# Cross-attention on one Trainium2 core: the products for the maxima made from three of six partial products, two heads in the two halves of TensorE's rows

## What is computed

```python
qh, kh, vh = split_heads(q @ wq.T + bq), split_heads(k @ wk.T + bk), split_heads(v @ wv.T + bv)   # 16 heads of 16
scores = einsum('bhqd,bhkd->bhqk', qh, kh) / sqrt(16)        # 512 queries, 1024 keys
attn = softmax(where(mask == 0, -1e9, scores))
out = einsum('bhqk,bhkd->bhqd', attn, vh) ... @ wo.T + bo
```

## Time and profile before

| | us |
|---|---|
| median of 3 runs | 1036.03 |
| lowest and highest | 1030.18, 1039.89 |
| the profiled execution | 1033.9 |
| its span, first to last instruction | 1032.1 |
| PE busy, all stages | 909.1 (88%) |
| DVE busy | 644.1 (62%) |
| ACT busy | 468.8 (45%) |
| POOL busy | 321.6 (31%) |
| c stage, from its first DMA issue (141.5) to the next stage's (400.8) | 259.3 |
| h stage, likewise (726.8 to 899.4) | 172.6 |

### The profile page before, as it was taken

How to read it: one execution, slowest core, us unless ns; L and a number is a source line. 1 busy time by engine, 2 the same in 40 slices (tenths; PEclk the granted TensorE clock), 3 DMA queues, 4 the chain that set the end, 5 groups by cost and what they waited for, 6 DMA issues and landing times. The chain is left out here.

```text
span 1032.1 us, 12736 instructions
## 1 busy us (share of the span) xinstructions
PE 909.1 (88%) x4040; PEld 460.9 (45%) x4044; DVE 644.1 (62%) x1329; ACT 468.8 (45%) x926; POOL 321.6 (31%) x328
## 2 busy tenths in 40 slices
PE   5879888999999986599799999999979998639986
PEld 2435553333333235366655555555422332434565
DVE  4855667888899824455145555654698996545464
ACT  3776444677777761022133333332207777133321
POOL 7325536300000000265235454553320000116633
PEclk9989998999999997699799999999988999859998
DMA  5040036033224704433590000000200000093100
GB/s 150 1 152 1 1 67 97 1 48 48 48 48 104 270 1 144 191 123 103 173 388 0 1 1 1 0 1 1 77 3 17 32 17 1 24 341 111 32 16 25
DMA packets 41654, 73.77 MB, mean 71 GB/s; under 512 B 8965, under 2 KB 27781, under 8 KB 40437
## 3 DMA queue, kind: packets, MB, share of 16 engines
q1 hardware_dynamic: 36372, 59.68, 19.4%
q0 software_dynamic: 4400, 13.11, 3.9%
q10 hardware_dynamic: 816, 0.17, 0.1%
HBM read 49.67 MB, written 10.49 MB: 58 GB/s over the span
## 5 line engine op out<-in xcount | busy, mean ns | idle before, releaser
L1066 DVE TENSOR_REDUCE c_amx<-PS 128x1 f32<-128x512 f32 x256 | 158.7, 682 | 29.9 <-PE PS L966 29.7
L1158 ACT ACTIVATE c_aE<-PS 128x512 f32<-128x512 f32 x256 | 132.5, 602 | 47.0 <-PE PS L978 46.9
L1782 POOL TENSOR_SCALAR s_Pn<-s_Pr,s_rs 128x512 f32<-128x512 f32 x64 | 100.1, 1567 | 107.4 <-DVE s_rs L1810 107.2
L68 POOL TENSOR_SCALAR rstd<-mv 128x4 f32<-128x4 f32 x8 | 1.9, 233 | 342.7 <-DVE mv L91 342.6
L966 PE MATMUL PS<-c_aKs,c_aQs 99*128 99x512 bf16 x256 | 95.8, 386 | 6.6 <-DMA c_aQs<-area 3.5
L978 PE MATMUL PS<-c_aQs,c_aKs 99*128 99x512 bf16 x256 | 94.5, 380 | 3.5 <-ACT c_aE L1158 2.3
L1869 ACT ACTIVATE s_Pr<-PS,s_nmx 128x512 f32<-128x512 f32 x64 | 44.0, 688 | 116.2 <-DVE s_nmx L1803 116.2
L1801 DVE TENSOR_REDUCE s_mx<-PS 128x1 f32<-128x512 f32 x64 | 44.2, 691 | 69.0 <-PE PS L1917 69.0
L1066 DVE TENSOR_REDUCE h_amx<-PS 128x1 f32<-128x512 f32 x128 | 79.7, 682 | 9.1 <-PE PS L966 8.8
L1158 ACT ACTIVATE h_aE<-PS 128x512 f32<-128x512 f32 x128 | 67.9, 600 | 23.6 <-PE PS L978 23.2
L989 PE MATMUL PS<-c_aE,c_VB 128*17 128x512 f32 x512 | 67.4, 598 | 0.1
(11 more groups left out here) (438 smaller groups left out, 1686.3 us busy)
## 6 DMA issues: line engine op xcount, KB each, us to landing
area<-in_e_w SPq DMA_DIRECT2D x16, 512.0 KB, 9.4
area<-in_g_w SPq DMA_DIRECT2D x8, 1024.0 KB, 16.4
c_aKs<-area SPq DMA_DIRECT2D x48, 128.0 KB
g_B<-in_g_b SPq DMA_DIRECT2D x1, 4096.0 KB, 16.2
c_aQs<-area SPq DMA_DIRECT2D x48, 64.0 KB
h_aQs<-h_QP SPq DMA_DIRECT2D x48, 64.0 KB
early<-in_ctxT SPq DMA_DIRECT2D x2, 1024.0 KB, 8.1
e_B<-in_e_b SPq DMA_DIRECT2D x1, 2048.0 KB, 11.3
```

The source lines that it names most:

```text
L1066: dve.tensor_reduce(self.mx[:, qt, j, half:half + 1], PS[:, n % MB, :], AX.X, ALU.max).then_inc(self.max_done, 1)
L1158: act.activation(self.E[kt % 2][:, j, :], PS[:, MB + x % XB, :], ACT.Exp, scale=0.25).then_inc(self.exp_done, 1)
L1782: pool.tensor_scalar(Pn[g % NPB][:, :], Pr[g % NPB][:, :], rs[:, g % NPB:g % NPB + 1], None, ALU.mult).then_inc(pn_ready, 1)
```

## The change

`Qs` and `Ks` become 115 rows high, and there are two layouts (`STACKS`). Heads 0 and 1 of a unit use the first, with the three partial products of slots 0, 3 and 4 and the tails in rows 0 to 50 and the rest up to row 98. Heads 2 and 3 use the second, with the same in rows 64 to 114, the others in rows 16 to 63 and zeros in rows 0 to 15. `scores` contracts only rows 0 to 50 or 64 to 114. It takes the heads in the order 0, 2, 1, 3 and issues them in pairs ahead of two `transposed_scores`, which contract 99 or 115 rows. Every DMA for the tails, keys and queries becomes two, one for each layout, with half of the partitions (32 instead of 64) and two heads. POOL sets the zero rows at the start of each stage. In the h stage the keys are laid out twice: DVE makes 9 copies instead of 2 after the splitting, PE 8 transposes instead of 4, ACT one copy of 1024 columns instead of 512. `MB` and `XB` are as before. What is left is the order of heads and dimensions in the weights (`dim_major`), which costs nothing on the chip.

```diff
+class Stack:
+    def __init__(self, slots, tail, main, rows):
+        self.slots, self.tail, self.main, self.rows = slots, tail, main, rows
+    def slot(self, n):
+        return slice(self.slots[n], self.slots[n] + HD)
+STACKS = (Stack((0, 35, 51, 16, 67, 83), slice(32, 35), slice(0, 51), slice(0, 99)),
+          Stack((64, 99, 16, 80, 32, 48), slice(96, 99), slice(64, 115), slice(0, 115)))
+PAIR = 2
+ROWS = 115
+HEAD_ORDER = (0, 2, 1, 3)
...
+def pair_rows(g, t):
+    first = g % 2 * 64 + t * 32
+    return slice(first, first + 32)
@@ Attention.tensor
-        def scores(u, c, j):
-            n = (u * C + c) * GH + j
+        def scores(u, c, i):
+            n = (u * C + c) * GH + i
+            j = HEAD_ORDER[i]
+            rows = stack_of(j).main
...
             if n >= MB:
                 pe.wait_ge(self.max_done, n - MB + 1)
-            pe.matmul(PS[:, n % MB, :], self.Qs[u % self.NQ][:, j, qt * P:(qt + 1) * P],
-                      self.Ks[self.key_buffer(u)][:, j % self.KH, half * BANK:(half + 1) * BANK],
+            pe.matmul(PS[:, n % MB, :], self.Qs[u % self.NQ][rows, j, qt * P:(qt + 1) * P],
+                      self.Ks[self.key_buffer(u)][rows, self.key_head(j), half * BANK:(half + 1) * BANK],
                       start=True, stop=True).then_inc(self.s_done, 1)
...
                 for j in range(GH):
-                    if v is not None:
-                        scores(v, c, j)
+                    if v is not None and j % PAIR == 0:
+                        for i in range(j, j + PAIR):
+                            scores(v, c, i)
                     transposed_scores(u, kt, j)
...
+    def set_zeros(self, pool, stacks, n):
+        for t in stacks:
+            pool.memset(t[0:HD, pair_heads(1), 0:n], 0.0).then_inc(self.zeros_set, 1)
@@ Attention.vector
-            for j in range(GH):
-                n = (u * C + c) * GH + j
+            for i, j in enumerate(HEAD_ORDER):
+                n = (u * C + c) * GH + i
@@ cross_stage, SP
             def key_part(u, p):
                 b, g = divmod(u, NG)
-                src = KP[p][g % 2 * 64:g % 2 * 64 + 64, b, g // 2, :]
                 for slot in KEY_SLOTS[p]:
-                    sp.dma_start(at.Ks[u % 3][slot * HD:(slot + 1) * HD, :, :], src).then_inc(at.loaded[u % 3], 16)
+                    for t, stack in enumerate(STACKS):
+                        sp.dma_start(at.Ks[u % 3][stack.slot(slot), pair_heads(t), :],
+                                     KP[p][pair_rows(g, t), b, g // 2, :]).then_inc(at.loaded[u % 3], 16)
@@ cross_stage, POOL
+            at.set_zeros(pool, at.Qs, S)
+            at.set_zeros(pool, at.Ks, NK)
@@ hard_cross_stage, POOL
-            pool.memset(KS[:, :, TAIL:TAIL + 2], 1.0).then_inc(ends_set, 1)
-            pool.memset(KS[:, :, TAIL + 2:ROWS + 1], 0.0).then_inc(ends_set, 1)
+            pool.memset(KS[:, :, :, :], 0.0).then_inc(ends_set, 1)
+            pool.wait_ge(ends_set, 2)
+            for t, stack in enumerate(STACKS):
+                first = stack.tail.start
+                pool.memset(KS[:, t, :, first:first + 2], 1.0).then_inc(ends_set, 1)
+            at.set_zeros(pool, at.Qs, S)
@@ hard_cross_stage, DVE, take_found
+                own.link(dve.tensor_tensor(third, KR[:, i, :], second, ALU.subtract))
+                for p, part in enumerate((first, second, third)):
+                    for t, stack in enumerate(STACKS):
+                        for slot in KEY_SLOTS[p]:
+                            if (t, slot) != (0, p):
+                                dve.tensor_copy(KS[:, t, i, stack.slot(slot)], part).then_inc(ks_ready, 1)
@@ hard_cross_stage, PE, found_keys
-                for i in range(TB):
-                    last = pe.transpose(key_bank(b)[:, i * P:(i + 1) * P], KS[:, b * TB + i, 0:ROWS], sh.identb[:, :])
+                for t in range(len(STACKS)):
+                    for i in range(TB):
+                        last = pe.transpose(key_bank(b)[:, t * S + i * P:t * S + (i + 1) * P], KS[:, t, b * TB + i, 0:ROWS],
+                                            sh.identb[:, :])
```

More of the change, by code:

```diff
@@ L972, in transposed_scores @@
             n = (u * KT + kt) * GH + j
+            rows = stack_of(j).rows
+            if u == 0 and kt == 0 and j == 0:
+                pe.wait_ge(self.zeros_set, self.zeros)
             if kt == 0:
@@ L977, in transposed_scores @@
                 pe.wait_ge(self.exp_done, n - XB + 1)
-            pe.matmul(PS[:, MB + n % XB, :], self.Ks[self.key_buffer(u)][:, j % self.KH, kt * P:(kt + 1) * P],
-                      self.Qs[u % self.NQ][:, j, :], start=True, stop=True).then_inc(self.st_done, 1)
+            pe.matmul(PS[:, MB + n % XB, :], self.Ks[self.key_buffer(u)][rows, self.key_head(j), kt * P:(kt + 1) * P],
+                      self.Qs[u % self.NQ][rows, j, :], start=True, stop=True).then_inc(self.st_done, 1)
         def values(u, kt):
@@ L3194, in layouts @@
     one = 0x3F80
[L3195 removed]
+    A["q_tail"] = np.repeat(np.array([[0], [0], [one]], np.uint16), PAIR * S, 1)
     A["ctxT"] = I["ctx_1024"].transpose(2, 0, 1).reshape(KD, P, -1).transpose(1, 0, 2)
```

75 lines of the change are left out of this document (41 added, 34 removed).

## The result

The changed kernel takes 1067.57 us (median of 4 runs, 1064.56 to 1068.48), the kernel before 1037.09 (4 runs): 1.030 times as long, 95% interval 1.024 to 1.035. The forecast was 1072, its own range 1062 to 1080. The profiled execution took 1068.48 us, its span is 1066.7, so 34.6 more than the span before.

The account below looks back on a forecast made before the run. PE sets the pace, with DVE 0.33 us a step to spare. Terms 13.9 + 1.7 + 9.5 + 8.6 + 2.3 = 36.0 on 1033.9 gave 1069.9, with 2.1 for the median 1072; own range 1062 to 1080, with rivals 1047 to 1084.

Parts of the forecast that it names:

- The chain of the three banks: Plain step: fourth product waits for the step's first maximum, starts at t + 1.17; step 3.00 us instead of 2.81.
- Overlap of the pairs, and a turn of 0.107: Products for the maxima: paired products run side by side; each switch between row layouts costs PE 0.107 us.
- Steps, 13.9: c and h steps: 50 on-time steps 9.0 us, 32 late ones 3.2, 16 new turns 1.7; 13.9 in all.
- Prologue of the c stage, 1.7: c prologue: same chain, two turns more for each of eight, 1.7 us.
- Start of the c stage, 9.5: c start: 24 issues at an unchanged 0.64 us each move the whole stage by 9.5 us.
- Waits for loads, 8.6: Later c units: loads take 20.8 us including 3.1 to land, exceeding their windows; PE waits 8.6 us.
- the forecast's sign of waits in units 1 to 5: c stage: DMA waits of 0.5 to 3 us expected ahead of the last steps of units 1 to 5.
- The h stage's one-offs, 2.3: h keys: seven more DVE copies and a link, four more transposes, ACT's longer copy; 2.3 us for two batches.
- halved issues: Rival, SP's DMAs: an issue with half the partitions costs half; 1056 us, chance 0.15.
- No overlap: Rival, products for the maxima: pairs do not run side by side, 7 us more; 1079 us, chance 0.08.
- DVE's pace: Rival, plain steps: fourth product not held, DVE sets the pace; 1024 us with halved issues, else 1040 or more; chance 0.06.
- Turns and issues both cheap: Rival, steps and DMAs: chain right, but layout turns and DMA issues cost little; 1045 us, chance 0.05.

Follow-up runs that it names:

- e5_half_max_after: Changed kernel with each maximum taken over 256 of the 512 columns of its product; 1050.26 us.
- e3_three: Changed kernel with the step order pair, three transposed products, pair, one transposed product, values; 1059.37 us.
- e6_half_max_before: Kernel before the change with each maximum taken over 256 of the 512 columns of its product; 1022.75 us.
- e1_full_rows: Changed kernel with the products for the maxima contracting all 99 or 115 rows, order in pairs kept; 1059.06 us.
- e4_late_zeros: Changed kernel with POOL's memsets moved behind the work DVE does at the start of a stage; 1061.93 us.
- e10_best: Changed kernel with the order of e3_three, the zeros of e4_late_zeros, and the second layout's loads of units 0 and 3 to 7 issued from POOL; 1056.06 us.
- e11_held: e10_best with the semaphores for POOL's DMAs taken ahead of all stages; 1057.17 us.
- e13_first_zeros: e11_held with full rows, maxima and transposed products by turns, and the first buffers' zeros set ahead; 1045.94 us.

## Why the prediction was right, step by step

- *The chain of the three banks* (fourth product at t + 1.17, plain step 3.00). Right: 1.17 and 3.01 in the profile; e5_half_max_after freed it by DVE alone (2.75), e3_three by the order alone (2.80), and e6_half_max_before showed that it didn't bind before.
- *Overlap of the pairs, and a turn of 0.107.* Right: two products in 0.39, and 0.32 from a pair to the transposed products in after, where e1_full_rows has 0.22 between the same matmuls. "TensorEngine Tiling (Array Packing)" of the Trainium skill, Key Properties, has a change of tiling mode drain the engine. The rows show 0.10 to 0.11 a turn, in the first stage and in the c stage, less than waiting for a matmul of 0.39 to end would cost; the measurement decides here.
- *Steps, 13.9.* Measured 13.1: 10.7 in the c steps less 1.3 of waits for loads, and 3.7 in the h steps (4.9 less 1.2 in the first, which belongs to the second batch's keys). Plain steps gave 0.20 instead of 0.18, but there are only 31 of 2.81 or 2.82 in the kernel before and not 50, so they gave 6.1 and not 9.0. The others gave 7.0 where 3.2 and 1.7 were forecast: the late steps, taken at 0.1 of 0 to 0.32, gave 0.01, 0.11, 0.12 and 0.30, and the four with late values 0.30 each. That the term came out is partly luck.
- *Prologue of the c stage, 1.7.* Measured 2.7. One round takes 3.41 instead of 3.12, 0.30 for two turns and what they push, where two turns at 0.107 were 0.21. The rest is at its ends.
- *Start of the c stage, 9.5.* Measured 9.1: an issue of 32 partitions takes 0.64 as one of 64 does. Within it two errors cancel, which is luck. The landing, from the end of SP's last issue to PE's load, was 1.46 instead of 3.1, and SP waited 1.2 for the first parts, since DVE was held back.
- *Waits for loads, 8.6.* The term that was mis-sized. Only the last steps of units 4 and 5 were longer than in the other units, by 0.8 and 0.5, so 1.3. The windows were right (20.45 for unit 3, forecast 20.35) and so was SP's time (18.55 with its slow issues, forecast 17.7). Wrong were the 3.1 to land, read off the start of the stage. The last step of unit 4, in after:

```profile
328.61 1.23 SPq L1478 DMA_DIRECT2D c_aQs<-area  x2
...
331.23 0.10 PEld L998 LDWEIGHTS PS<-c_aKs,c_aQs 51*128 51x128 bf16 x2 [1.70 <-DMA c_aQs<-area]
```

SP's last issue ended at 329.84, the load went 1.39 later. In the last steps of units 1 to 3 the loads still had 0.5 to 1.0 to spare, so the forecast's sign of waits in units 1 to 5 came for two of the five. A wait that the profile puts down to a DMA need not cost anything: of the 1.70 here 0.85 is there in every plain step.
- *The h stage's one-offs, 2.3.* Measured 6.3: 5.1 at the start and 1.2 in the first step. The doubled keys account for some 2 of it, as forecast; 4.1 are POOL's memsets against DVE, a term that had been given "0 to 2" and counted as 0. e4_late_zeros took 4.1 away. The h stage as a whole is 8.2 longer, where the sign said 6.
- The rest, +2.1, is scatter of untouched parts.

Sum of the measured terms: 13.1 + 2.7 + 9.1 + 1.3 + 6.3 = 32.5, forecast 36.0. So the chain, the overlap and the cost of an issue were right, and the total of 1067.6 stands as near to 1072 as it does by luck as well: two terms missed in opposite directions, 7.3 too much and 4.0 too little, and the untouched parts added 2.1. The rivals: halved issues (1056) fell with the row of six issues in 3.86. No overlap (1079) fell with the pair in 0.39. DVE's pace (1024 or 1040) fell with the fourth product at t + 1.17. "Turns and issues both cheap" (1045) fell with both.

## What to carry to other kernels

Before a matmul is made shorter, look for what the next one waits for: with three banks and a maximum of 0.62, the fourth product starts 1.17 after the first whatever PE saves, and all that is moved behind it goes onto the path. Changing the layout so that each DMA moves half as much doubles the queue's time, because an issue costs the same 0.64; and a queue with little room left turns what is won in the steps into waits (5.9 of 7.6 us in e3_three). A memset on an idle engine is free only if no neighbour shares its way to memory: look at what runs beside it, not only at what its own engine does next.

## What the hardware showed that I had not expected

**POOL's memsets and DVE.** All instructions of the normalising line, in after and before, and of POOL's zeros in after. Columns: durations min/median/max in ns, first and last start.

```profile
L1538 DVE TENSOR_SCALAR X<-X,mv,rstd x8: 396/1080/1966, 143.3 to 152.6; 128x256 f32<-128x256 f32 x8
```

```profile
L1491 DVE TENSOR_SCALAR X<-X,mv,rstd x8: 394/398/652, 141.5 to 145.3; 128x256 f32<-128x256 f32 x8
```

```profile
L1092 POOL MEMSET c_aQs<- x3: 941/1085/1088, 143.3 to 145.2; 16x1024 bf16 x3
L1092 POOL MEMSET c_aKs<- x3: 1934/1934/1936, 146.2 to 150.0; 16x2048 bf16 x3
```

DVE's instruction alone takes 398 ns. Beside the memsets its median is 1080 and its longest 1966. Five of the eight start 0.04 to 0.12 us after a memset has started and end some 0.15 after it ends, so each of these waits for a whole one (1085 and 1934). The memsets lose as well: three take 3.01 beside DVE and 2.72 alone (e4_late_zeros). DVE's instructions that read PSUM are not slowed: those behind the first normalising take 1.39 for two in e3_three, with a memset running, and 1.40 in e4_late_zeros without one. The page "SBUF — State Buffer" of the Trainium skill, section "SBUF: two separate sides", has DVE and GpSimd share a pair of ports under an exclusive lock, held for the whole instruction; of DVE's instructions with one SBUF input it says so for those in a 2-port mode. The rows agree with the lock; which mode these instructions were in, no row shows.

**Issues from POOL are cheaper than from SP, and a stage's end is dearer.** 0.50 against 0.64 us an issue for the same DMA, and 7 us at the end of the stage in the four kernels that did it. What takes them is open.

**TensorE's clock at a stage's start.** The stretches of the first products before (2 us each, columns as above):

```profile
157.00:159.00 2.00, 1.68 (x4) 0.60 (x5) 1.06 (x2) 0.00 (x0) 1.10 (x1) 0.50 1.03 143
...
163.00:165.00 2.00, 1.65 (x7) 0.67 (x5) 1.92 (x4) 1.97 (x4) 2.00 (x2) 1.00 0.04 4
```

PE had been idle ahead of them, and its granted clock is 0.50 (1.2 GHz) there and 1.00 (2.4 GHz) some 6 us later. How soon it rises differs between executions and moves the c prologue and the h steps by up to 3 us, as much as a small change is worth. e10_best and e11_held have the same order of PE's work and prologues of 38.0 and 41.0: the clock rose 6.2 and 11.3 after the first product, and in e11_held it was low once more from 199.2 to 202.6. With the two layouts it rose 4.7 to 11.3 after the first product in the eight executions with pairs, 3.0 to 3.2 in three with full rows, and in e13_first_zeros it had not fallen; in the two of the kernel before and its half maxima it rose after 5.5 and 6.2. One execution of each is too few to say what decides it.
